# A gated attention unit and a state-space stage, four batches in a hardware loop against four batches unrolled and interleaved

## The chip, the core and the metric

The kernel runs on one core of one Trainium2 chip. Its time is the device time of one execution in microseconds (us). The core has five engines with instruction streams of their own, which meet only at semaphores: TensorE (PE) multiplies matrices into PSUM, VectorE (DVE) and ScalarE (ACT) work element by element, GpSimd (POOL) does some element work too, and SyncE (SP) issues transfers. PE loads weights in a side stream (PEld).

## The reference, cut to what matters

The program chains six blocks on a residual tensor of 4 batches x 1024 tokens x 128 channels. The change touches the third and the fifth. Both normalise twice, and the result of the first normalisation is added to the residual.

```python
x = attention(x); x = x + moe(norm(x))            # blocks 1 and 2, not touched
# block 3, gated unit, per batch b
n = norm(x[b]); x2 = norm(n)                      # the block's own layernorm is the second
u, v, base = split(silu(x2 @ uv_w.T + uv_b))      # 256, 256 and 128 channels
q, k = rope(base * gamma + beta)                  # two affine copies, rotated
kern = relu(q @ k.T / sqrt(128) + toeplitz(w)) ** 2      # 1024 x 1024
x[b] = x[b] + n + (u * (kern @ v)) @ o_w.T + o_b
x = x + moe(norm(x))                              # block 4, not touched
# block 5, state space, per batch b, 16 states
n = norm(x[b]); x2 = norm(n)
xs, z = split(x2 @ W_in.T)                        # 256 channels each
u = silu(causal_conv(xs, 4 taps))
dt, B, C = split(u @ W_xproj.T)                   # 16 + 16 + 16
delta = softplus(dt @ W_dt.T + b_dt)
h[s, t] = exp(delta[t] * A[s]) * h[s, t-1] + delta[t] * B[s, t] * u[t]   # per state s
y = sum_s C[s] * h[s] + D * u
x[b] = x[b] + n + (y * silu(z)) @ W_out.T
# block 6: gated feed-forward, attention, gated feed-forward, not touched
```

## The kernel before

Channels of a block lie on the 128 partitions while it is computed (256 channels are two tiles, c = 0 and 1); the 1024 tokens of a batch run along the free axis, in two halves of 512 (g), since a PSUM bank holds 512 numbers. All eight PSUM banks are one tile `ps`. Most matmuls are float32 and are recorded as two passes of the array, so `x8` in a row of PE is four matmuls.

**Order.** Nothing is scheduled by a planner. Each block has one function per engine, the instructions stand in the order in which the function writes them, and each engine waits on named semaphores (`sm[...]`). Both blocks run in a hardware loop over the four batches (`Fori`, lines 2131 to 2260 build it per engine). At the end of a turn each engine reports to `batch_done`, SP waits for all of them, clears every semaphore of the stage and lets them go on (`finish`, `clear`). So nothing of batch b+1 starts before batch b is wholly done.

**Gated unit** (`pe_gau` L808, `act_gau` L857, `dve_gau` L880, `pool_gau` L931). DVE normalises twice (`dve_layernorm` L82: statistics L79, variance L91, a root on POOL L100, the subtraction and scaling L94), then adds to X (L885, L886). PE transposes eight token tiles (L107), ACT copies them out (L114), PE projects base (L814), gate u (L818), the rotated base (L823) and value v (L827). ACT applies silu (L861, L865) and the two affine copies (L869, L873); DVE adds the bias of v (L889), ACT takes its silu (L877), DVE rotates q and k (L893 to L897). Then come 16 steps u, two for each block j of 128 keys: PE scores (L838), DVE adds the Toeplitz bias (L903) and squares the positive part (L906), and PE multiplies by v (L844), one j behind the scores. At the end DVE gates (L912), PE projects out (L852) and DVE adds to X tile by tile (L921).

**State space** (`pe_mamba` L1267, `act_mamba` L1345, `dve_mamba` L1385, `pool_mamba` L1453). It has the same two normalisations and L1390 for the addition to X, the projections (PE L1274), copies (ACT L1349, L1352), the convolution (DVE L1394, L1398), silu (ACT L1355), low-rank dt and B, C in two matmul groups (PE L1280, L1285), copies of them (ACT L1357, L1359), a split of B and C into three bf16 parts (DVE L1403 to L1407), D*u (DVE L1410), delta (PE L1292, ACT L1362 to L1367, DVE L1415 to L1420). Then 16 states. In each, DVE multiplies by B for c = 0 (`drive`, L1426), POOL for c = 1 (L1465), ACT makes the decays (L1379), DVE scans (L1433, twice) and multiplies by C (L1438, twice), and PE spreads B and C (L1314, L1326) and sums y in PSUM (L1308, `add_y`). `drive` of state n+1 stands right behind the products of state n. POOL's product for a state waits for the scans of the state before and for the sum that frees its buffer. At the end: gate (L1448), output projection (L1340), addition (L921).

## Time and profile before

| | us |
|---|---|
| median of 3 runs (3761.12 to 3766.71) | 3764.24 |
| the profiled execution: its time | 3772.41 |
| the profiled execution: its span | 3769.2 |
| PE busy | 2795.5 (74%) |
| DVE busy | 2229.2 (59%) |
| ACT busy | 1601.7 (42%) |
| POOL busy | 707.9 (19%) |

The blocks follow one another, so the busy shares are averages over stages with different limits. The gated unit lies from 1594 to 1948 us of the span, the state-space stage from 2225 to 3043 us. Together they are 1172 us. A time that an engine sits idle in them counts only where nothing else on the path is running.

### The profile page before, as it was taken

The numbers are of one execution on the slowest core, as the hardware profiler recorded it, in microseconds if no ns is written. First come the engines' busy times: TensorE is split into PE (matmuls) and PEld (weight loads), VectorE is DVE, ScalarE is ACT, GpSimd is POOL, SyncE is SP. The second block draws the span as 40 slices with busy tenths as digits, with TensorE's granted clock in tenths as the row PEclk, the third lists the DMA queues.
The fourth block names the chain that finished last, engine by engine and source line by source line (L and its number), as shares of the span: only waits on it lengthen the run. The fifth ranks groups of instructions, "written<-read, shape, count | busy, mean of one in ns | idle before, by whom it ended". The sixth has DMA issues, their size and how long they took to land.

```text
span 3769.2 us, 55186 instructions
## 1 busy us (share of the span) xinstructions
PE 2795.5 (74%) x18720; PEld 1601.4 (42%) x18720; DVE 2229.2 (59%) x4893; ACT 1601.7 (42%) x2886; POOL 707.9 (19%) x926
## 2 busy tenths in 40 slices
PE   2998899899899926367762636666665688888888
PEld 1666566566566626333332622222222253233225
DVE  2564555455456431355553238889796988777754
ACT  1665566476466502111100314242433333666672
POOL 2000000000000064300016332212121221222221
PEclk9999999999999958688875867778777798999998
DMA  5000000000000011100001210000000034011000
GB/s 157 1 0 2 1 0 1 2 1 0 2 1 0 12 39 52 39 0 0 0 4 39 60 28 0 0 0 0 0 0 0 0 116 157 2 47 47 2 2 23
DMA packets 65897, 78.75 MB, mean 21 GB/s; under 512 B 9005, under 2 KB 41948, under 8 KB 65712
## 3 DMA queue, kind: packets, MB, share of 16 engines
q1 hardware_dynamic: 56816, 60.10, 4.9%
q0 software_dynamic: 8896, 16.29, 1.6%
q8 instruction: 102, 1.67, 0.2%
q14 instruction: 83, 0.68, 0.1%
HBM read 43.58 MB, written 35.52 MB: 21 GB/s over the span
## 4 chain that ended last, share of the span: by engine, by line
PE 28%; DVE 15%; issue 13%; POOL 4%; another core or an unknown queue 3%; ACT 2%; DVEq 0%; DMA 0%; POOLq 0%; SPq 0%; ACTq 0%
DVE Wqkv L1737 4%; PE ps L1613 3%; PE ps L844 3%; PE ps L971 2%; PE ps L590 2%; PE ps L838 2%; PE ps L579 2%; DVE arena L1433 2%; PE ps L1585 1%; DVE arena L1438 1%; POOL arena L1465 1%; PE ps L1574 1%; PE ps L980 1%; POOL slots_in L749 1%
## 5 line engine op out<-in xcount | busy, mean ns | idle before, releaser
L431 DVE CUSTOM_DVE_ANT_0 arena<-ps,causal 128x512 f32<-128x512 f32 (+3 forms) x512 | 282.7, 589 | 345.3 <-PE ps L247 343.8
L355 ACT ACTIVATE arena<-ps 128x512 f32<-128x512 f32 (+1 forms) x640 | 337.8, 548 | 321.7 <-PE ps L260 318.9
L368 ACT ACTIVATE arena<-arena 128x640 f32<-128x640 f32 (+7 forms) x512 | 393.8, 770 | 36.7 <-DVE arena L431 32.7
L1737 DVE TENSOR_REDUCE Wqkv<-ps 128x2 f32<-128x1024 f32 (+3 forms) x384 | 353.3, 953 | 87.1 <-PE ps L1578 81.7
L260 PE MATMUL ps<-ident,arena 128*128 128x128 f32 x2304 | 359.5, 283 | 46.1 <-ACT arena L368 44.6
L1693 ACT ACTIVATE arena<-ps 128x1024 f32<-128x1024 f32 (+3 forms) x384 | 302.3, 809 | 163.0 <-PE ps L1585 159.3
L281 PE MATMUL ps<-arena,rope 128*64 128x128 f32 x4608 | 350.5, 282 | 0.0
L1433 DVE TENSOR_TENSOR_SCAN arena<-arena 128x1024 f32<-128x1024 f32 x128 | 318.9, 2532 | 9.2 <-ACT arena L1379 4.7
L260 PEld LDWEIGHTS ps<-ident,arena 128*128 128x128 f32 x2304 | 249.0, 141 | 177.0 <-issue 144.2
L1308 PE MATMUL ps<-arena,ident 128*128 128x512 f32 x512 | 281.7, 702 | 0.0
L281 PEld LDWEIGHTS ps<-arena,rope 128*64 128x64 f32 x4608 | 242.3, 136 | 74.8 <-issue 64.1
L1465 POOL TENSOR_TENSOR arena<-arena 128x1024 f32<-128x1024 f32 x64 | 150.6, 2353 | 553.4 <-PE ps L1308 218.7
L508 POOL COPY arena<-arena 128x512 f32<-128x512 f32 x64 | 39.5, 616 | 1055.0 <-DVE arena L455 1055.0
L247 PE MATMUL ps<-arena 64*128 64x512 bf16 (+3 forms) x2304 | 233.5, 327 | 5.1 <-ACT rope L347 5.1
L1375 ACT ACTIVATE arena<-ps 128x1024 f32<-128x1024 f32 x64 | 65.5, 1023 | 318.3 <-PE ps L1314 318.3
L1314 PE MATMUL ps<-arena,select 96*128 96x512 bf16 x128 | 51.9, 497 | 182.3 <-DVE arena L1426 182.3
L1308 PEld LDWEIGHTS ps<-arena,ident 128*128 128x128 f32 x512 | 120.7, 236 | 142.6 <-issue 132.7
L1613 PE MATMUL ps<-arena,W 128*32 128x512 f32 (+3 forms) x1536 | 164.5, 500 | 7.2 <-POOL arena L1764 3.6
L763 POOL DMA_INDIRECT arena<-slots_out,arena x128 | 128.2, 1002 | 197.0 <-DMA slots_out<-arena 88.2
L714 DVE TENSOR_SCALAR arena<-ps,b1T 128x160 f32<-128x160 f32 x128 | 42.6, 379 | 203.6 <-remote 112.4
L1585 PE MATMUL ps<-arena 64*128 64x512 bf16 (+3 forms) x768 | 124.8, 334 | 46.4 <-DVE Wqkv L1737 39.5
L100 POOL TENSOR_TENSOR rstd<-var_eps,minus_half 128x8 f32<-128x8 f32 x28 | 46.2, 1650 | 554.4 <-DVE var_eps L91 440.1
(259 smaller groups left out, 4824.0 us busy)
## 6 DMA issues: line engine op xcount, KB each, us to landing
arena<-q_dram SPq DMA_DIRECT2D x4, 2048.0 KB, 8.8
arena<-k_dram SPq DMA_DIRECT2D x4, 2048.0 KB, 14.1
q_dram<-arena SPq DMA_DIRECT2D x24, 256.0 KB, 3.7
k_dram<-arena SPq DMA_DIRECT2D x24, 256.0 KB, 3.8
arena<-slots_in SPq DMA_DIRECT2D x8, 640.0 KB, 4.5
slots_out<-arena SPq DMA_DIRECT2D x8, 640.0 KB, 3.9
slots_in<-arena POOLq DMA_DIRECT2D x4, 640.0 KB, 7.9
W<-in_m_W_dram SPq DMA_DIRECT2D x1, 2048.0 KB, 9.9
```

What stands on the lines that cost most here:

```text
L247: mm = nc.tensor.matmul(k.ps[:, banks[h], 0:w], q, kk, start=part == 0, stop=part == 2)
L260: mm = nc.tensor.transpose(k.ps[:, 4 + m % 2, (b - b0) * P:(b - b0 + 1) * P], k.prob[:, n % 2, h, j * P:(j + 1) * P], k.ident[:])
L281: mm = nc.tensor.matmul(k.ps[64 * h:64 * h + 64, 6 + n // 4, (n % 4) * P:(n % 4 + 1) * P], k.v_tok[:, parity, j, 64 * h:64 * h + 64], k.pr ...
L355: nc.scalar.activation(k.probT[:, n % 2, b0 * P:(b0 + nb) * P], k.ps[:, 4 + m % 2, 0:nb * P], ACT.Copy)\
L368: nc.scalar.activation(k.prob[:, i % 2, h, 0:w], k.prob[:, i % 2, h, 0:w], ACT.Exp, bias=k.neg_max[:, i % 2, h:h + 1], scale=-1.0, accum_o ...
L431: ins = nc.vector.tensor_tensor_reduce(k.prob[:, i % 2, h, 512 * g:512 * g + w], k.ps[:, banks[h], 0:w], k.causal[:, first:first + w], 1.0 ...
L1308: mm = nc.tensor.matmul(k.ps[:, 4 + 2 * c + g, :], k.ident[:], k.h[:, 2 * m + c, g * 512:(g + 1) * 512], start=False, stop=last)
L1433: nc.vector.tensor_tensor_scan(h, k.da[:, 2 * m + c, :], h, 0.0, ALU.mult, ALU.add).then_inc(sm["scan"], 1)
L1465: nc.gpsimd.tensor_tensor(k.h[:, 2 * m + 1, :], k.du[:, 1, :], k.b_row[:, m, :], ALU.mult).then_inc(sm["dbx1"], 1)
L1613: mm = nc.tensor.matmul(k.ps[32 * r:32 * r + 32, 6, 512 - w:512], k.v_aug[b % 2][:, j, 4 * Q + r, :], k.expT[:, (2 * s + a) % 4, h, 0:w], ...
L1693: nc.scalar.activation(k.expT[:, n % 4, :, 0:w], k.ps[:, 2 * (m % 3):2 * (m % 3) + 2, 0:w], ACT.Exp, scale=-1.0)\
L1737: nc.vector.tensor_reduce(k.least[:, g, a, i % 4, c, :], k.ps[:, 2 * (m % 3):2 * (m % 3) + 2, 0:search_width(i, c)], AX_X, ALU.min)\
```

## The change

The hardware loops over batches of the two blocks are gone. Each engine's function now contains all four batches in one straight stream, semaphore counts go on over batches, and there is one `finish` per block. Within that stream:

- The two normalisations of batch b+1 are cut into 16 pieces (`dve_norm_piece`; pieces 3 and 9 are empty, and 14, 15 and, in the state-space stage, 13 hold nothing). Piece n stands behind step n of batch b on DVE. POOL's two roots stand behind states 3 and 9.
- PE transposes and projects batch b+1 around its last sums of batch b; ACT and DVE follow with its copies, rotation or convolution. The output projection of batch b now stands behind projections of b+1.
- Results are added to X in two operations of 512 columns instead of eight of 128, and the output projection waits for all four gated pieces at once.
- State space: dt, B and C come from one group of matmuls (112 rows of weights); D*u moves from DVE to ACT; softplus's logarithm, the addition and the product are done per half. `h`, `conv`, `ud`, `xs` and `XN2s` lie in the space of weights that are no longer needed, and z is double buffered.

Main parts of the diff:

```diff
+def dve_norm_piece(nc, k, dve, ch, sm, b, piece, out):
+    if piece in (0, 1, 6, 7):
+        for t in range(4 * (piece % 2), 4 * (piece % 2) + 4):
+            last = nc.vector.bn_stats(k.bn6[:, t, :], (k.X_all[:, 8 * b + t, :] if piece < 2 else k.XN[:, t, :]))
+        ch.link(last)
+    elif piece in (2, 8):
+        for t in range(8):
+            last = nc.vector.bn_aggr(k.mv[:, t, :], k.bn6[:, t, :])
+        ch.link(last)
+        nc.vector.tensor_scalar(k.var_eps[:], k.mv[:, :, 1], EPS, None, ALU.add).then_inc(sm[("var1", "var2")[piece // 8]], 1)
+    elif piece in (4, 5, 10, 11):
+        dve.wait_ge(sm[("rstd1", "rstd2")[piece // 10]], b + 1)
...
+    elif piece == 12:
+        X = k.X_all[:, 8 * b:8 * b + 8, :]
+        ch.link(nc.vector.tensor_tensor(X, X, k.XN[:], ALU.add))
...
 def pe_gau(nc, k, pe, sm):
...
+    for b in range(k.B):
+        for j in range(8):
+            scores(b, j)
+            if j >= 1:
+                mix(b, j - 1)
+        if b + 1 < k.B:
+            pe.wait_ge(sm["biased"], 16 * b + 14)
+            pe_tokens(nc, k, pe, sm, b + 1, k.XN2)
+        mix(b, 7)
+        if b + 1 < k.B:
+            base(b + 1)
+            gate(b + 1)
+            rotated(b + 1)
+        results(b)
+        if b + 1 < k.B:
+            value(b + 1)
...
 def dve_gau(nc, k, dve, ch, sm):
...
+    def prepare(b):
+        for c in range(2):
+            dve.wait_ge(sm["affine"], 4 * b + c + 1)
+            ch.mark(nc.vector.tensor_tensor(k.gaff[:, c, :], k.gaff[:, c, :], k.cos[:], ALU.mult))
+        for c, dst in enumerate((k.gq, k.gk)):
+            dve.wait_ge(sm["affine"], 4 * b + 3 + c)
+            ch.link(nc.vector.tensor_tensor(k.gaff[:, 2 + c, :], k.gaff[:, 2 + c, :], k.sin[:], ALU.mult))
+            nc.vector.tensor_tensor(dst[:], k.gaff[:, c, :], k.gaff[:, 2 + c, :], ALU.add).then_inc(sm["qk"], 1)
+        if b >= 1:
+            add_results(b - 1)
+        dve.wait_ge(sm["v_ps"], b + 1)
...
             nc.vector.scalar_tensor_tensor(k.kern[:, j, g * 512:(g + 1) * 512], tmp, 0.0, tmp, ALU.max, ALU.mult)\
                 .then_inc(sm["kern"], 1)
-        dve.wait_ge(sm["kern"], u + 1)
+            if b + 1 < k.B:
+                norm_piece(b + 1, u)
...
 def pe_mamba(nc, k, pe, sm):
...
+        if b + 1 < k.B:
+            pe.wait_ge(sm["dbx0"], 16 * b + 16)
+            pe.wait_ge(sm["b"], 16 * b + 16)
+            pe_tokens(nc, k, pe, sm, b + 1, k.XN2s)
+            project(b + 1, 0)
+        add_y(b, NSTATE - 1)
+        if b + 1 < k.B:
+            project(b + 1, 1)
+            project(b + 1, 2)
+            project(b + 1, 3)
+        results(b)
...
 def dve_mamba(nc, k, dve, ch, sm):
...
+    for b in range(k.B):
+        split_bc(b)
+        step_size(b)
+        drive(b, 0)
+        for n in range(NSTATE):
+            step(b, n)
+            if n + 1 < NSTATE:
+                drive(b, n + 1)
+            if b + 1 < k.B:
+                dve_norm_piece(nc, k, dve, ch, sm, b + 1, n, k.XN2s)
+        if b + 1 < k.B:
+            convolve(b + 1, 0)
+        gate(b)
+        if b + 1 < k.B:
+            convolve(b + 1, 1)
+        add_results(b)
...
 def pool_mamba(nc, k, pool, sm):
...
+            if n in (3, 9) and b + 1 < k.B:
+                pool_norm_root(nc, k, pool, sm, b + 1, n // 9)
...
-            with pe.Fori(5, 5 + B) as b:
-                use_batch(k, b - 5)
-                pe_gau(nc, k, pe, k.G)
-                finish(b)
+            pe_gau(nc, k, pe, k.G)
+            finish(5)
```

The end of a batch on PE in the gated unit, before: the last scores and products, the output projection, and the end of the loop's body, whose next turn begins with L107.

```order
L838 MATMUL ps<-arena 128x512 x2
L844 MATMUL ps<-arena 128x512 x8
L852 MATMUL ps<-owT,arena 128x128 x16
L2154 REGISTER_ALU
L2164 REGISTER_ALU
L2164 COMPARE_AND_BRANCH
```

And of the change, where L903 are scores, L912 products with v, L850 the next batch's transposes, L869, L877, L884 and L890 its base, gate, rotated base and value, and L922 the output projection:

```order
L903 MATMUL ps<-arena 128x512 x2
L912 MATMUL ps<-arena 128x512 x4
L850 MATMUL ps<-ident,arena 128x128 x8
L912 MATMUL ps<-arena 128x512 x4
L869 MATMUL ps<-XNT,uvT 128x512 x2
L877 MATMUL ps<-XNT,uvT 128x512 x4
L884 MATMUL ps<-arena,rotate 128x512 x2
L922 MATMUL ps<-owT,arena 128x128 x16
L890 MATMUL ps<-uvT,XNT 128x256 x8
L903 MATMUL ps<-arena 128x512 x4
```

The transposes went ahead of the last four products, three projections ahead of the output projection, and the value projection behind it.

Two states on DVE in the state-space stage, before (a scan is named by its operands here, L1433; L1438 are the products with C, L1426 is `drive`):

```order
L1433 SCALAR_TENSOR_TENSOR arena<-arena 128x1024
L1438 TENSOR_TENSOR arena<-arena,ps 128x1024 x2
L1423 REGISTER_ALU
L1425 ISA
L1426 TENSOR_TENSOR arena<-arena,ps 128x1024
L1430 REGISTER_ALU
L1433 SCALAR_TENSOR_TENSOR arena<-arena 128x1024
```

And of the change, states 1 and 2 of a batch (L1585 scans, L1590 products, L1576 `drive`):

```order
L1585 SCALAR_TENSOR_TENSOR W<-arena,W 128x1024 x2
L1590 TENSOR_TENSOR W<-W,ps 128x1024 x2
L1576 TENSOR_TENSOR W<-arena,ps 128x1024
L816 BN_STATS bn<-X 128x6 x4
L1585 SCALAR_TENSOR_TENSOR W<-arena,W 128x1024 x2
L1590 TENSOR_TENSOR W<-W,ps 128x1024 x2
L1576 TENSOR_TENSOR W<-arena,ps 128x1024
L820 BN_AGGR mv<-bn 128x2 x8
L822 TENSOR_SCALAR var_eps<-mv 128x8
L1585 SCALAR_TENSOR_TENSOR W<-arena,W 128x1024 x2
```

A piece of the next batch's normalisation now stands between `drive` and the next scans.

From the last state of one batch to the first of the next on DVE, of the change (before, L1448 and L921 closed the batch and everything else of these rows stood behind the barrier):

```order
L1590 TENSOR_TENSOR W<-W,ps 128x1024 x2
L1526 TENSOR_SCALAR W<-Wqkv,conv_w 128x1024
L1530 SCALAR_TENSOR_TENSOR W<-Wqkv,conv_w,W 128x1024 x3
L1537 TENSOR_TENSOR W<-ps,arena 128x512 x4
L1526 TENSOR_SCALAR W<-Wqkv,conv_w 128x1024
L1530 SCALAR_TENSOR_TENSOR W<-Wqkv,conv_w,W 128x1024 x3
L1544 TENSOR_TENSOR X<-X,ps 128x512 x2
L1549 TENSOR_TENSOR arena<-ps,arena 32x1024 x2
```

The next batch's convolution (L1526, L1530) now lies on either side of this batch's gate (L1537), ahead of its addition to X (L1544).

## Rows read from the trace of the kernel before

**Rows 1.** Busy time in four stretches: length, PE, PEld, DVE, ACT, POOL; PE clock.
```profile
1675.00:1763.46 88.46, 63.72 (x168) 31.37 (x168) 47.68 (x106) 13.82 (x12) 3.27 (x2) 0.85 0.00 0
1725.00:1764.00 39.00, 38.46 (x90) 16.72 (x88) 19.54 (x29) 0.00 (x0) 0.00 (x0) 1.00 0.00 0
2286.23:2419.88 133.65, 86.98 (x183) 34.37 (x182) 132.50 (x79) 47.35 (x46) 35.33 (x16) 0.79 0.00 0
2419.88:2490.95 71.07, 41.31 (x100) 16.87 (x99) 38.91 (x83) 23.07 (x21) 5.67 (x4) 0.73 0.00 0
```
**Rows 2.** Timeline of DVE, gated unit, second batch: start, busy, [idle before <-releaser].
```profile
1682.70 1.64 DVE L79 BATCH_NORM_STATS2 bn<-X 128x6 f32 x8 [1.00 <-SPq L2058]
...
1686.97 2.14 DVE L94 TENSOR_SCALAR XN<-X,mv,rstd 128x128 f32 x8 [1.75 <-POOL rstd L100]
...
1695.47 1.23 DVE L885 TENSOR_TENSOR X<-X,XN 128x1024 f32 x1
...
1709.67 2.48 DVE L889 TENSOR_TENSOR arena<-ps,uvb_row 128x512 f32<-128x512 f32 x4 [11.71 <-PE ps L827]
...
1716.72 2.36 DVE L897 TENSOR_TENSOR arena<-arena 128x1024 f32<-128x1024 f32 x2
```
**Rows 3.** Timeline of PE, gated unit, second batch.
```profile
1693.83 2.27 PE L107 MATMUL ps<-ident,arena 128*128 128x128 f32 x8 [12.46 <-DVE arena L94]
1696.96 3.78 PE L814 MATMUL ps<-XNT,uvT 128*128 128x512 f32 x4 [0.87 <-ACT XNT L114]
...
1719.14 6.56 PE L838 MATMUL ps<-arena 128*128 128x512 f32 x8 [9.59 <-DVE arena L897]
...
1756.43 7.03 PE L844 MATMUL ps<-arena 128*128 128x512 f32 x16
...
1766.40 3.44 PE L852 MATMUL ps<-owT,arena 128*128 128x128 f32 x24 [0.33 <-DVE X L921]
```
**Rows 4.** Timeline of ACT, gated unit, second batch.
```profile
1700.79 1.11 ACT L861 ACTIVATE arena<-ps,uvb 128x1024 f32<-128x1024 f32 x1 [2.57 <-PE ps L814]
...
1705.43 2.36 ACT L869 ACTIVATE arena<-arena,g_cols 128x1024 f32<-128x1024 f32 x2
...
1712.19 1.91 ACT L877 ACTIVATE arena<-arena 128x2048 f32<-128x2048 f32 x1 [2.20 <-DVE arena L889]
```
**Rows 5.** Timeline of DVE, a step of the first batch.
```profile
1641.63 0.69 DVE L903 SCALAR_TENSOR_TENSOR arena<-ps,toeplitz 128x512 f32<-128x512 f32 x1 [2.28 <-PE ps L838]
```
**Rows 6.** Timeline of DVE, state space, end of batch one to scans of batch two.
```profile
2417.55 2.33 DVE L1438 TENSOR_TENSOR arena<-arena,ps 128x1024 f32<-128x1024 f32 x2
...
2449.41 0.81 DVE L1394 TENSOR_SCALAR arena<-arena,conv_w 128x1024 f32<-128x1024 f32 x1 [5.25 <-ACT arena L1349]
2450.26 3.93 DVE L1398 SCALAR_TENSOR_TENSOR arena<-arena,conv_w 128x1024 f32<-128x1024 f32 x3
...
2471.09 2.47 DVE L1403 TENSOR_TENSOR arena<-ps,arena 32x1024 f32<-32x1024 f32 x2 [12.21 <-ACT arena L1359]
...
2490.95 4.47 DVE L1433 TENSOR_TENSOR_SCAN arena<-arena 128x1024 f32<-128x1024 f32 x2 [1.17 <-ACT arena L1379]
```
**Rows 7.** Timeline of DVE and POOL, two states of the first batch.
```profile
2395.99 4.47 DVE L1433 TENSOR_TENSOR_SCAN arena<-arena 128x1024 f32<-128x1024 f32 x2
...
2403.00 2.35 POOL L1465 TENSOR_TENSOR arena<-arena 128x1024 f32<-128x1024 f32 x1 [7.97 <-PE ps L1308]
...
2403.94 5.74 DVE L1433 TENSOR_TENSOR_SCAN arena<-arena 128x1024 f32<-128x1024 f32 x2
```
**Rows 8.** Timeline of PE, the sums of one such state, and the low-rank matmuls.
```profile
2404.77 3.60 PE L1308 MATMUL ps<-arena,ident 128*128 128x512 f32 x8
...
2460.02 6.37 PE L1280 MATMUL ps<-arena,WxT 128*16 128x512 f32 x8 [6.43 <-ACT arena L1355]
```
**Rows 9.** Timeline of ACT, a table load and the exponential of softplus.
```profile
2475.83 1.28 ACT L1365 ACT_TABLE_LOAD   x1
2477.13 1.91 ACT L1365 ACTIVATE arena<-arena 128x2048 f32<-128x2048 f32 x1
```

734 lines of the change are left out of this document (390 added, 344 removed).

## The prediction, made before the changed kernel was timed

> **What bounds the kernel now.** I read the profile by stages first, because the page's shares mix blocks with different limits. Busy time by stretch [rows 1] shows one period of the gated unit, from the end of one batch's products with v to the next: 88.46 us, of which PE is busy 63.7 and DVE 47.7. Inside its 16 steps PE is busy 38.5 of 39 us at a granted clock of 1.00. So the steps are bound by PE, and the rest of the period is a chain through all engines. The state-space stage is the opposite: in its 16 states DVE is busy 132.5 of 133.65 us, and between the last products of one batch and the first scan of the next lie 71.07 us with DVE busy only 38.9. Then I read the timelines of these gaps to see which wait ends last.
>
> Gated unit [rows 2, 3]: DVE normalises from 1682.7 to 1697.9, PE sits 12.46 us until the first normalised tile, DVE then sits 11.71 us for the value matmuls, and PE 9.59 us for the rotated q and k. State space [rows 6]: DVE waits 5.25 us for the projections and 12.21 us for the low-rank ones. Those are the waits that the change can take away.
>
> **Gated unit, one transition.** Unit costs. PE at full clock takes 7.03 us for 16 passes of 512 columns [rows 3], near 0.43 each: base 1.7, gate 3.4, rotation 1.7, value 3.4 (eight 256-column matmuls, taken as the same number of columns), scores of one j 1.7, its products 3.4. Transposes 2.3, output projection 3.44 for 24 of 32 passes, so 4.6 [rows 3]. ACT takes 1.1 per 1024 columns and 1.9 for v [rows 4]. DVE takes 2.48 for four 512-column pieces, 1.2 per 1024-column product [rows 2], and 1.45 per step, two operations of 0.69 and the gap between them [rows 5].
>
> Let K be the end of a batch's products. The transposes and their copies lie ahead of K, behind products of 3.4. Then PE: base until K+1.7; the gate needs three of four gated pieces, K+1.9 to 5.3; rotation 7.0; output projection 11.6; value 15.1. ACT: base 2.9, two affine copies 5.3, u 7.5, the rotated copies 8.6 and 9.7. DVE: gated 2.5, cosine products 6.5, the sine products and additions end at 13.4, additions to X 14.8, bias of v 17.5; ACT's silu of v ends at 19.5. PE meanwhile does the scores of j = 0 and 1 until 18.5, so it idles about 1 us for v. I add 1 us for the second key half, whose step on DVE waits behind the bias of v and a piece. From there PE needs 3.4 for the first products and 5.15 for each j; the eight products, the seven scores still between them and the transposes end at K+59.6.
>
> Do the pieces delay it? DVE's pieces here are the 15.25 us between 1682.7 and 1697.95, less two root waits of 1.75 [rows 2], about 12 us, at most 2.5 per j beside 2.9 of steps. Only one j reaches 5.4 against PE's 5.15, and DVE has lead by then (it idles 2.28 in each j now [rows 5]). Cost nothing; if that cover is gone, up to 12 us per batch. The roots fall in a step's shadow. The period falls from 88.5 to 59.6: 28.9 x 3 = 87. In the first batch q and k are prepared ahead of v's bias: about 7 less of PE's 9.6 idle. The output projection at the very end no longer streams with the gate: 1 more. **Gated unit: -93.**
>
> **State space, one transition.** E is the end of the last products, 2419.88; the next scan is at E+71.1 [rows 6]. After: PE does tokens and the first projection ahead of the last sum, done at about E+2.4; ACT's copy E+3.5; convolution of c = 0 takes 0.81 and 3.93 [rows 6], 8.2; gate 2.5, 10.7; convolution of c = 1, 15.4; silu 16.5. PE: last sum 5.9, three projections 11.1, output projection 15.7, low rank 19.1 (one group of 3.4 where there were two). ACT: D*u is done by 18.7, dt copy 20.1. PE: delta 21.9 and 23.6. ACT: absolute values 24.7, a table load and the exponential of 1.28 and 1.91 [rows 9], 28.0, another load and the first logarithm, 30.4. DVE: addition and product for both halves, four of 1.2, 35.3; `drive` 36.6. POOL's product started at 35.4 and takes 2.35; it holds the scan as described next, until 37.7. Gain 71.1 - 37.7 = 33.4. The split of B and C, the other long DVE item (it begins near 21.1), ends before the logarithm does.
>
> **State space, the 16 states.** DVE is the limit, so pieces are not free. A state without a disturbance is 7.95 us from scan to scan (2395.99 to 2403.94 [rows 7]). Every second one is longer: its two scans take 5.74 instead of 4.47, while POOL's product, started at 2403.00 after 7.97 us of waiting for PE's sum, still runs until 2405.35, 1.4 us into them [rows 7]. PE is late there because it ran part of that sum at the lower clock: the mean over the states is 0.79 [rows 1], the undisturbed sum takes 3.60 [rows 8]. From first scan to last product 15 x 7.95 + 6.8 = 126 would remain of 133.65; 7.6 are this contention. A piece of 0.8 to 1.2 between `drive` and the scan moves the scan behind POOL's product: two neighbouring pieces add over 1.4 in most states. So the pieces add their work, some 11 us (the gated unit's 12 without L886), and take back about 5.6 of the 7.6 (what is left sits at the empty pieces and the last states). The two roots on POOL, 1.6 each (DVE waits 1.75 for one now [rows 2]), may collide with scans: between 0 and 3.3, I take 1.6 since either may start first; two scaling pieces may meet POOL's product, 0.9. Sum: 126 + 11 + 2 + 1.6 + 0.9 = 141.5, that is 7.9 more. Net per transition 33.4 - 7.9 = 25.5, three of them 76.5; the last batch has no pieces.
>
> The Trainium skill ("SBUF — State Buffer", Who interferes with whom) says that a DVE instruction with two SBUF inputs, or one in a 2-port mode, and a GpSimd instruction that reads SBUF exclude each other for the whole instruction, whoever starts first. The lengthening of 1.27 for 1.41 us of overlap agrees. By that rule a root that starts first holds the scan for all its 1.6 us, against this change: both would always cost, 3.3 a batch, 5 us more in all than my sum.
>
> First batch: from its silu the same chain as above, 60.6 us from start to scan now; the merged low-rank matmuls (6.37 for the first group at the lower clock [rows 8]) and the halves of softplus save about 8.5. The end loses 1.3 like the gated unit. **State space: 76.5 + 8.5 - 1.3, so -83.7.** Everything else (blocks 1, 2, 4 and 6) is as before; the barriers' 1 us each are inside the periods.
>
> **Sum.** 93 + 83.7 = 176.7. The profiled execution, 3772.4 with 3.2 us around its span, would be 3596; it is 8.2 above the median, so the median goes from 3764.2 to **3588**.
>
> **Rivals.** (a) The scans stay held. If every state of the three batches loses 1.27, not only a few, each has 20.3 instead of 2: 3 x 18.3 = 55, so 3643. For it: PE idles longer per state with pieces in it, and its clock was already low in every second state. Against: the pieces shift the scans. 12%. (b) The lower clock in the transitions: 17 us of matmuls per gated transition and 8.5 on the path in state space, doubled, 3 x 25.5 = 77: 3665. For: the matmuls behind idle times of 9 to 12 us are slow now (6.56 for eight passes [rows 3]). Against: idle times before them shrink to 1 or 2 us. 6%. (c) DVE becomes the gated unit's bound and each piece is exposed, 12 x 3 = 36: 3624. 5%. (d) It doesn't overlap as it says: only normalisations, transposes and the barrier leave the path (1681.7 to 1697.0, 15.3 us in either stage [rows 2, 3]), since the next projections wait for this batch's banks. Then each gated transition gains 13.6 less and each of state space 18.1 less: 3 x 31.7 = 95, 3683. 4%. (e) Slower: PE, busy without a pause, is granted only the lower of its two levels, 1.2 GHz, through the gated unit. Its matmuls per batch (41.2 of steps, 17.1 of the rest, 58 us) double: four times 58 = 232 against the gain of 177, 3820. It decides from 76% of that work at the lower level. Against: 1.00 over 39 us of unbroken work [rows 1]. 3%.
>
> **How the numbers follow.** My forecast, 68% (2% are left for what I don't see): its own bounds are -6 for a gated period with no idle at all, -14 if nothing collides in the states, and +19 if the collisions stay as they are (5.6 x 3, with the second root), +15 for hops and leads I took as free: 3568 to 3622. The range takes in (c) and most of (a), to hold 8 in 10: 3566 to 3643. Under 0.2% (7.5 us) a measurement can hardly tell from no change. Faster: all but (e) and a little unknown, 0.95; same 0.01; slower 0.04.
>
> **What would show it.** Gated unit: period near 60, PE idle before the first products 1 to 2 us, clock near 1.00 throughout. State space: first scan 36 to 39 us behind the last product; scans of 4.5 per pair in most states with pieces; a period near 179 against 204.7. The forecast is wrong if DVE idles beyond 2 us for PE in the gated steps, if pairs of scans of 5.7 stay in every second state, or if another chain than silu, low rank and softplus ends last between batches.

## The result and the profile after

The changed kernel took **3555.4 us** (median of 4 runs, 3552.0 to 3556.6) against 3764.1 of the kernel before in the same session: 0.9444 of it, 95% interval 0.9428 to 0.9461. The forecast was 3588 with a range from 3566 to 3643. The direction and the mechanism were right; the gain is 209 us where 177 were forecast, and the time lies 11 us below the range. The same program, timed again in a later session, took 3563.2 (`after_again` below), 3 us below the range.

The profiled execution took 3556.6 (span 3554.6). PE, DVE, ACT and POOL busy, against 2795.5, 2229.2, 1601.7 and 707.9 before:

```profile
PE 2724.2 (77%) x18688; PEld 1583.0 (45%) x18688; DVE 2196.1 (62%) x4845; ACT 1599.9 (45%) x2891; POOL 717.9 (20%) x923
```

The number of matmul passes is nearly the same (18720 before), and PE is busy 71 us less. TensorE's granted clock has two levels in these traces, 1.00 (2.4 GHz) and 0.50 (1.2 GHz). Eight passes of 512 columns take 3.60 us at the full level and about 7.2 at the lower one (the row of after_again at the end of this text); a time between the two means that the level changed on the way, and a granted clock between the two is a mean over a stretch. Less of PE's work ran at the lower level after the change, and most waits went. Busy time by stretch, the answer to [rows 1] (length, PE, PEld, DVE, ACT, POOL, clock): a period of the gated unit, the states of the second batch, its transition to the third (last product to first scan), and the states of the last batch, which hold no pieces:

```profile
1666.84:1724.90 58.06, 56.51 (x170) 28.56 (x169) 45.78 (x100) 11.14 (x10) 3.27 (x2) 1.00 0.00 0
2342.57:2479.85 137.28, 86.69 (x196) 35.52 (x197) 136.56 (x130) 48.30 (x48) 43.64 (x18) 0.85 0.00 0
2479.85:2513.29 33.44, 26.42 (x78) 12.01 (x78) 26.27 (x27) 24.16 (x22) 1.10 (x1) 0.85 0.00 0
2683.98:2819.58 135.60, 88.01 (x185) 35.12 (x186) 134.05 (x79) 46.44 (x45) 36.55 (x16) 0.79 0.00 0
```

The gated unit is now bound by PE, 56.5 of 58.06 us. The transition fell from 71.07 to 33.44. The states rose by 3.6 only, though 11 pieces went into them; and the last batch, without pieces, is hardly shorter.

Where the 214.6 us between the two profiled spans are, from the boundaries of the stages on DVE:

| stretch | before | after | gain | forecast |
|---|---|---|---|---|
| up to the gated unit (block 2 is 281.5 / 277.8 of it) | 1594.9 | 1591.1 | 3.9 | 0 |
| gated unit | 353.3 | 256.7 | 96.6 | 93 |
| block 4 | 277.5 | 273.4 | 4.1 | 0 |
| state space | 818.5 | 710.1 | 108.4 | 83.7 |
| the rest | 725.0 | 723.3 | 1.7 | 0 |

PE in the second transition of the gated unit, the answer to [rows 3] (L850 transposes, L912 products with v, L869, L877, L884 and L890 base, gate, rotation and value, L922 output projection):

```profile
1720.43 1.04 PE L850 MATMUL ps<-ident,arena 128*128 128x128 f32 x8
1721.30 3.60 PE L912 MATMUL ps<-arena 128*128 128x512 f32 x8
...
1726.88 3.70 PE L877 MATMUL ps<-XNT,uvT 128*128 128x512 f32 x8 [0.26 <-DVE arena L1021]
...
1732.13 3.73 PE L922 MATMUL ps<-owT,arena 128*128 128x128 f32 x32
...
1744.05 1.13 PE L912 MATMUL ps<-arena 128*128 128x512 f32 x2 [1.29 <-ACT arena L970]
```

The waits of 12.46 and 9.59 us in [rows 3] are now one of 1.29. The eight transposes take 1.04 where 2.27 stood.

The transition from the second to the third batch of state space, E = 2479.85, all engines (L1526 and L1530 convolution, L1537 gate, L1374 low rank, L1490 copy of dt, L1386 delta, L1563 the first addition of softplus, L1585 scans):

```profile
2479.43 1.02 ACT L1479 ACTIVATE Wqkv<-ps 128x1024 f32<-128x1024 f32 x1 [2.07 <-PE ps L1366]
2480.49 0.81 DVE L1526 TENSOR_SCALAR W<-Wqkv,conv_w 128x1024 f32<-128x1024 f32 x1 [0.64 <-ACT Wqkv L1479]
...
2485.18 2.48 DVE L1537 TENSOR_TENSOR W<-ps,arena 128x512 f32<-128x512 f32 x4
...
2493.49 1.97 PE L1374 MATMUL ps<-arena,WxT 128*112 128x512 f32 x4 [0.16 <-ACT arena L1485]
2495.53 1.02 ACT L1490 ACTIVATE arena<-ps 16x1024 f32<-16x1024 f32 x1
2496.60 3.80 PE L1386 MATMUL ps<-arena,WdtT 16*128 16x512 f32 x8 [1.15 <-ACT arena L1490]
...
2507.17 1.23 DVE L1563 TENSOR_TENSOR arena<-arena 128x1024 f32<-128x1024 f32 x1 [1.89 <-ACT arena L1500]
...
2513.29 3.40 DVE L1585 TENSOR_TENSOR_SCAN W<-arena,W 128x1024 f32<-128x1024 f32 x1
```

E is again the end of the last product. DVE waits 0.64 us for the projection where it waited 5.25 [rows 6]. The chain through silu, low rank and softplus ends last, as forecast, but it starts at E+0.6, not E+3.5.

DVE, POOL and PE in the states, the answer to [rows 7, 8]: first a state with a piece, then the fourth state, whose scans have a root on POOL beside them, then a held pair of scans in the last batch (L816 a piece, L842 a root, L1632 POOL's product, L1405 the sum):

```profile
2351.44 0.86 DVE L816 BATCH_NORM_STATS2 bn<-X 128x6 f32<-128x128 f32 x4
2352.33 4.47 DVE L1585 TENSOR_TENSOR_SCAN W<-arena,W 128x1024 f32<-128x1024 f32 x2
...
2369.52 4.47 DVE L1585 TENSOR_TENSOR_SCAN W<-arena,W 128x1024 f32<-128x1024 f32 x2
...
2369.69 3.55 POOL L842 TENSOR_TENSOR rstd<-var_eps,minus_half 128x8 f32<-128x8 f32 x1 [1.72 <-DVE var_eps L822]
...
2694.67 5.28 PE L1405 MATMUL ps<-W,ident 128*128 128x512 f32 x8
...
2700.12 2.36 POOL L1632 TENSOR_TENSOR W<-arena 128x1024 f32<-128x1024 f32 x1 [8.08 <-PE ps L1405]
...
2700.98 5.83 DVE L1585 TENSOR_TENSOR_SCAN W<-arena,W 128x1024 f32<-128x1024 f32 x2
```

With a piece the scans start behind POOL's product and take 4.47. Without pieces the old pattern is back. The root did not hold a scan: it began 0.17 us behind the first of the two and took 3.55 us itself, where one without a scan beside it takes 1.64.

### The profile page after: what moved, and what is told of

It reads as the page before. It is cut to its first block, busy times and chain, and to the rows that moved or that the text cites. A ratio compares the mean times of both kernels' runs of the same rounds, so it can differ in the third digit from the quotient of the medians.

```text
span 3554.6 us, 53842 instructions
## 1 busy us (share of the span) xinstructions
PE 2724.2 (77%) x18688; PEld 1583.0 (45%) x18688; DVE 2196.1 (62%) x4845; ACT 1599.9 (45%) x2891; POOL 717.9 (20%) x923
## 4 chain that ended last, share of the span: by engine, by line
PE 25%; DVE 17%; issue 13%; another core or an unknown queue 3%; ACT 3%; POOL 2%; DMA 0%; DVEq 0%; POOLq 0%; SPq 0%; ACTq 0%
DVE Wqkv L1902 4%; PE ps L1778 3%; PE ps L912 3%; PE ps L1070 2%; DVE W L1590 2%; PE ps L590 2%; DVE W L1576 2%; PE ps L579 2%; PE ps L1750 2%; PE ps L903 1%; PE ps L1739 1%; DVE W L1585 1%; POOL slots_in L749 1%; PE ps L1079 1%
## 5 line engine op out<-in xcount | busy, mean ns | idle before, releaser
L368 ACT ACTIVATE arena<-arena 128x640 f32<-128x640 f32 (+7 forms) x512 | 393.9, 770 | 36.8 <-DVE arena L431 33.3
L1585 DVE TENSOR_TENSOR_SCAN W<-arena,W 128x1024 f32<-128x1024 f32 x128 | 303.0, 2408 | 3.9
L1405 PE MATMUL ps<-W,ident 128*128 128x512 f32 x512 | 276.9, 692 | 0.0
L1632 POOL TENSOR_TENSOR W<-arena 128x1024 f32<-128x1024 f32 x64 | 150.6, 2353 | 497.4 <-PE ps L1405 203.6
L1405 PEld LDWEIGHTS ps<-W,ident 128*128 128x128 f32 x512 | 118.9, 232 | 137.9 <-issue 129.0
L1590 DVE TENSOR_TENSOR W<-W,ps 128x1024 f32<-128x1024 f32 x128 | 148.7, 1203 | 0.0
```

The lines of the kernel that those rows point to most:

```text
L368: nc.scalar.activation(k.prob[:, i % 2, h, 0:w], k.prob[:, i % 2, h, 0:w], ACT.Exp, bias=k.neg_max[:, i % 2, h:h + 1], scale=-1.0, accum_o ...
L1405: mm = nc.tensor.matmul(k.ps[:, 4 + 2 * c + g, :], k.ident[:], half(k.h[:, 2 * (n % 2) + c, :], g), start=False, stop=n == NSTATE - 1)
L1585: nc.vector.tensor_tensor_scan(h, k.da[:, 2 * (n % 2) + c, :], h, 0.0, ALU.mult, ALU.add).then_inc(sm["scan"], 1)
L1590: nc.vector.tensor_tensor(h, h, both(k.ps[:, 2:4, :]), ALU.mult).then_inc(sm["prod"], 1)
```

## Experiments

The runs fell on three chips. On two of them (13 and 14) blocks 2 and 4 take 206.0 to 208.9 us each in every kernel, on chip 9 273.4 to 281.5, and the kernel before takes 3624 and 3764. The other stages differ less (the gated unit of the change is 255.2 to 256.7, the part behind state space 723.2 to 725.1), so small effects are read from the length of a stage. The change itself was not run on 13 or 14. "The change" without a session means the 710.1 us of state space above, and "states" and "transition" are the two parts of a batch there: first scan to last product, and last product to the next batch's first scan.

### The two stages apart

`g_only` is the kernel before with the new functions of the gated unit and one `finish`; `s_only` is the changed kernel with the old ones and their loop.

> The gated unit of the change in the kernel before, state space as before. Theory (the two stages are independent, and the gated unit gave what the two traces show, 353.3 us before against 256.6 after): 3764 - 97 = 3667 us, and the second mixture-of-experts block behind it stays at 277.5 us. By the prediction's own term (93) it would be 3671. Rival: the 4.1 us by which that block was shorter in the changed kernel (273.4) belong to the unrolled gated unit in front of it; then 3663 and the block near 273.4.

> The state-space stage of the change with the gated unit as before. Theory: the stage takes 710 us instead of 818.5, so 3764 - 108 = 3656. By the prediction's own term (83.7) it would be 3680. Rival: what was gained beyond the forecast comes from one kernel's luck in alignment between stages, or from outside the stage; then between 3660 and 3680.

Measured in one session (before 3762.6): g_only 3670.9, ratio 0.9753 (0.9737 to 0.9769); s_only 3655.8, 0.9715 (0.9699 to 0.9731). The gains are 91.7 and 106.9, together 198.6. That is 10 us short of the 208.7 of the change, but it lies outside the two stages: these are 256.7 and 710.2 us long, as in the change. So they are independent, and most of the missed gain is inside state space. Block 4 is 276.1 with the new gated unit and 275.0 with the old one; in six later runs of kernels with the new one on this chip it is 273.5 to 276.5, and the change's own is 273.4 in its first session and 276.4 in after_again. So its 4.1 us, and block 2's 3.7, do not belong to the change: they vary from run to run.

### The cover taken away

```diff
# s_tokens_late                                  # state space, PE
-            pe_tokens(nc, k, pe, sm, b + 1, k.XN2s)
-            project(b + 1, 0)
         add_y(b, NSTATE - 1)
+            pe_tokens(nc, k, pe, sm, b + 1, k.XN2s)
+            project(b + 1, 0)
# g_pieces_late                                  # gated unit, DVE, behind the loop over u
-            if b + 1 < k.B:
-                norm_piece(b + 1, u)
+        if b + 1 < k.B:
+            for piece in range(14):
+                norm_piece(b + 1, piece)
```

> The changed kernel, but the next batch's transposes and first projection stand behind the last sum of the states instead of ahead of it. Theory: convolution begins 0.6 us after the last product now because tokens, copy and projection lie in the last state's shadow. Behind the sum they come one after another (sum until 3.0 us after the last product, transposes and first copy 2.1, projection 2.0, copy 1.1), convolution begins at 8.2, and nothing else covers it: 7.6 x 3 = 23 slower than 3555, 3578; with PE at its lower level there up to 3584. Rival: another chain (the gate, the output projection, the low-rank matmuls) ends late anyway and hides most of it; then under 10 slower, 3565 or less.

> The changed kernel, but in the gated unit the next batch's normalisation stands in one piece behind step 16 instead of one piece behind each step. Theory (the pieces cost nothing among the steps, because DVE idles there for PE): 13.5 us of pieces and two waits of 1.75 for a root are laid bare, less 3.6 that the products before the last cover, 13 us per batch, 39 in all: 3594, up to 3603 if PE falls to its lower level behind them. Rival: DVE was the bound in the steps with pieces, which cost about as much there as at the end; then within 12 of 3555.

s_tokens_late: 3588.7, 0.9536 (0.952 to 0.9552). The transition is 43.3 instead of 33.4, with E = 2491.20:

```profile
2495.42 1.04 PE L850 MATMUL ps<-ident,Wo 128*128 128x128 f32 x8
...
2500.64 0.81 DVE L1526 TENSOR_SCALAR W<-Wqkv,conv_w 128x1024 f32<-128x1024 f32 x1 [9.44 <-ACT Wqkv L1479]
```

Convolution starts at E+9.4, 8.8 us later than in the change, and the next scan comes 9.9 later: nothing hides the delay. The sum in front took 5.37 us for its eight passes, part of them at the lower level, which is the step from the expected 7.6 to 8.8. The last 1.1 are not in the start of the convolution: the output projection took 5.44 where the change has 3.80, and the low-rank matmuls stood behind it. The whole run is 33 us slower than the change, more than the expected 23 to 29. Of the 33.8 in state space 29.7 are the transitions and 3.6 the states, which are up to 2.4 us longer per batch; why was not followed up.

g_pieces_late: 3602.6, 0.9569 (0.9553 to 0.9585). The gated unit is 293.6 against 256.7, 12.3 per batch, as the forecast had it ("up to 12"), and DVE waits 1.75 for each root again, with PE idle. The whole run is 47 us above the change; besides these 37 us, 4.5 are a longer state-space stage (714.6, as in after_again, see "Not settled") and the rest lies in the untouched blocks. The transposes behind the idle time:

```profile
1743.72 2.05 PE L850 MATMUL ps<-ident,arena 128*128 128x128 f32 x8 [10.79 <-DVE arena L829]
```

So in the gated unit pieces are free among the steps. The transposes took 2.05 behind that idle time, 1.04 in the change.

### What holds the scans

```diff
# sum_split                                      # PE, in each state n
     for n in range(NSTATE):
+        if n >= 1: add_y(b, n - 1, (1,))        # c = 1 first
         if n + 1 < NSTATE: spread_b(b, n + 1)
         spread_c(b, n)
-        if n >= 1: add_y(b, n - 1)
+        if n >= 1: add_y(b, n - 1, (0,))
# drive waits for y_acc 2N - 2, POOL's product for 2N - 3
```

So POOL's product for c = 1 needs only the first half of PE's sum.

`before_sum_split` is the same edit in the kernel before.

> The changed kernel, but in each state PE sums the products of c = 1 first, then spreads B and C, then sums c = 0; POOL's product waits for the first half of the sum only. Theory (a scan is held because POOL's product starts late, and it starts late because PE, at 1.2 GHz after an idle time, ends the sum of eight passes behind the scans): every product of POOL now starts with the end of the scans and is over before the next ones. The last batch, which has no pieces, loses 8 holds of 1.2 (135.6 us from its first scan to its last product become 126 to 127.2), the three others 2.3 each: 15 to 16 us less than 3555, 3540. Rival 1: the lateness has another cause (the copy of B, the scans themselves): no change, 3555. Rival 2: spreading C later makes the products with C wait: slower, up to 3565.

> The kernel before with the same new order of PE's sums in the states (loops, barriers, everything else as before). Theory: 133.65 us of states become 126 to 127, four times 6.6 to 7.6: 3764 - 28 = 3736. If pieces were what really freed the scans in the change, and PE's order has no part in it, then no change: 3764. It also says what the pieces cost in truth: with the holds gone in both kernels they should cost their own 9 to 10 us per batch.

before_sum_split: 3594.2, 0.9915 (0.9899 to 0.9932) of 3623.9, 29.6 less. Its states of the second batch, and below them those of sum_split (last batch, second batch):

```profile
2336.94:2462.51 125.57, 86.45 (x183) 33.26 (x182) 124.43 (x79) 47.34 (x46) 35.44 (x16) 0.83 0.00 0
```

```profile
2552.51:2679.60 127.09, 81.13 (x185) 31.47 (x186) 125.54 (x79) 46.43 (x45) 36.63 (x16) 0.89 0.00 0
2209.28:2344.99 135.71, 84.80 (x191) 33.04 (x191) 134.99 (x130) 47.88 (x47) 43.69 (x18) 0.86 0.00 0
```

133.7 became 125.6 without any piece, and the last batch of the change 135.6 became 127.1. Each pair of scans takes 4.47 us now, but for the first of each batch in sum_split (5.57): the scans were held because POOL's product waited for PE's sum. With the holds gone the pieces show their real price, 135.71 - 127.09 = 8.6 us per batch. In the change they cost 1.7 beside the last batch (137.28 against 135.60), since they take the holds back.

But sum_split is only 3415.4, 0.9422 (0.9407 to 0.9438), and its stage 706.6: 3.5 us less where 15 to 16 were expected. The states gave back 13.2; the transitions took 7.9 (36.4, 37.8 and 34.0 instead of 33.4) and the end 1.8. Of the 7.9, about 2 only follow from where E lies: the last scans are no longer held (4.47 instead of 5.04), E comes 0.6 earlier, and PE's part does not, so convolution starts at E+1.3. The other 6 are PE's clock: in the second transition the half sums ahead of the transposes took 2.77 and 2.42 us instead of 1.98 and 1.88 (convolution at E+3.0), and delta took 6.12 and 5.86 us in the first two transitions where the change has 3.80:

```profile
2364.08 5.86 PE L1386 MATMUL ps<-arena,WdtT 16*128 16x512 f32 x8 [1.15 <-ACT arena L1492]
```

So part of the gain in the states was lost again to a lower clock of PE on the path. Whether it can be held up, the next runs ask.

### The order of the gate and a table load

```diff
# gate_last                                      # DVE
             convolve(b + 1, 0)
-        gate(b)
-        if b + 1 < k.B:
             convolve(b + 1, 1)
-        add_results(b)
+        gate(b)
# PE: results(b) and DVE: add_results(b) behind the next batch's delta
# exp_early                                      # ACT, behind the copy of B and C
+        nc.scalar.activation(k.warm[:], k.minus_half[:, 0:1], ACT.Exp)
```

> The changed kernel, but in the state-space stage this batch's gate (2.5 us of DVE) stands behind both halves of the next batch's convolution, and its output projection and addition to X behind delta. Theory: convolution, silu, low rank, delta and softplus are the chain that ends last between batches, and the gate lies on it with its whole 2.5 us: 3 x 2.5 = 7.4 less, 3548. Rival 1: another chain (sum, gate, output projection, addition to X) ends as late: no change, or slower by up to 3 x 3 = 9, since the output projection now stands ahead of the first B of the batch: 3555 to 3564.

> The changed kernel with one more ACT instruction per batch: an exponential of one column behind the copy of B and C, so that the table load of 1.28 us falls in ACT's idle 1.0 us before delta instead of between the absolute values and the exponential. Its result is not used. Theory: the chain through softplus is the last one; 1.28 is taken off it and the idle time before delta covers all of it but 0 to 0.5: 4 x 0.8 to 1.28 = 3.2 to 5.1 less, 3550 to 3552. Rival: the absolute value brings back another table, so the load returns where it was: no change or 5 slower, 3555 to 3560.

gate_last: 3419.6, 0.9433 (0.9418 to 0.9449); stage 710.2, transitions 33.4: no change. Its low-rank matmuls and the copy of dt were earlier, with 2.15 us of idle time of PE before the one and 1.11 behind them; delta started at E+15.0 instead of E+16.8, and then took 5.46:

```profile
2359.83 5.46 PE L1386 MATMUL ps<-arena,WdtT 16*128 16x512 f32 x8 [1.11 <-ACT arena L1493]
```

exp_early: 3417.3, 0.943 (0.9415 to 0.9446); stage 706.8. ACT's load lies under PE's delta, and the exponential of 1.91 follows the absolute value directly:

```profile
2189.31 1.28 ACT L1492 ACT_TABLE_LOAD   x1
2190.60 0.20 ACT L1492 ACTIVATE arena<-minus_half 128x1 f32<-128x1 f32 x1
...
2193.18 1.91 ACT L1498 ACTIVATE arena<-arena 128x2048 f32<-128x2048 f32 x1
```

The way to the first scan of the stage is 1.3 shorter, as expected, and the transitions are 32.6, 31.3 and 33.5. But delta took 5.14 in the third, and the states of the first three batches are 2.2 us longer in all (137.8, 138.9 and 137.4): from first scan to first scan the batches are 170.5, 170.2 and 170.9 long, where the change has 170.8, 170.7 and 170.7. So what the transitions gained was given back in the states; the 3.3 us of the stage are the 1.3 up to the first scan, 0.6 in these three batches and 1.4 in the states of the last one.

### PE's clock

Six kernels, counting the combinations, fill PE's idle time with matmuls whose result is zero or unused.

```diff
# warm: 32 rows, bf16, 8 passes behind each sum  # warm_rows: 128 rows, float32, 4 passes
+  nc.tensor.matmul(k.ps[:, 4 + i % 4, :], zeros32, zeros32, start=False, stop=False)
+  nc.tensor.matmul(k.ps[:, 4 + i % 4, :], k.ident[:], k.nil[:], start=False, stop=False)
# gate_last_warm: zeros of 32 rows               # gate_last_full: data, 128 rows
#   ahead of low_rank (8 or 4 passes) and ahead of delta (4 or 2)
# zeros32 stands for slices of rows 96 to 127 of `select`, which hold zeros
+  nc.tensor.matmul(k.ps[:, bank, :], zeros32, zeros32, start=True, stop=True)
+  nc.tensor.matmul(k.ps[:, bank, :], k.WinT[:, 0:P], half(k.XNT, 0), start=True, stop=True)
```

`all3` is warm, gate_last_warm and exp_early; `after_again` is the changed kernel beside them.

> The changed kernel itself, once more, on the same chip as the three runs beside it, so that differences of a few microseconds can be read directly. On the first chip it was 0.9444 of the kernel before. The other chip runs the two mixture-of-experts blocks 140 us faster for every kernel; if this is that chip, 3623.9 - 208 = 3416 and 0.943 to 0.944, with 710 us for the state-space stage.

> The changed kernel with matmuls of zeros in PE's idle time within the states: behind each state's sum 8 passes of 512 columns of zeros are added to the sums (20 in the first state). They change nothing in the result and add 1.7 us of work per state. Theory (every second sum runs at 1.2 GHz because PE idled 4 to 5 us before it, so POOL's product is late, and it holds the scan): with the idle time filled the clock stays at 2.4 GHz, the granted clock of the states rises from 0.85 and 0.79 to above 0.95, all sums take 3.6, the last batch's states fall from 135.6 to 127, the other three from 137.3 to 135.7, and the transitions stay at 33.4, since the last sums are at full clock anyway: 13 us less than the changed kernel beside it. Rival: the clock alternates whatever PE does, or zeros don't count as work: the passes then lengthen the slow states, 0 to 20 us more.

> gate_last (the gate behind both convolutions, the output projection behind delta) with matmuls of zeros into a free PSUM bank while PE waits for silu (8 passes) and for the copy of dt (4 passes). gate_last alone brought nothing: its second silu ended 1.9 us earlier behind the last product, but delta took 5.46 instead of 3.80 us at the lower clock. Theory (that clock swallowed the gain): delta is back at 3.8, transitions fall from 33.4 to about 31.5, three times 1.9, and the first batch, which has such a wait too, by up to 1: 5 to 7 us less than the changed kernel beside it. Rival: the output projection ahead of the first B of the batch, or the softplus chain of ACT, ends last now: within 2 of the changed kernel.

> The zeros in the states, gate_last_warm and exp_early together. If the three act on different terms (holds of scans 13, order of the gate 6, one table load 1.2 x 4 = 4.8) they add up: 24 us less than the changed kernel beside it. If the gate's order and the table load share one chain whose end is then DVE's split of B and C (it ended 1.2 us ahead of the logarithm in exp_early), 3 to 4 of it are lost: 20 less.

Measured on chip 9 (before 3764.4): after_again 3563.2, 0.9464 (0.9448 to 0.948); warm 3558.6, 0.9452 (0.9436 to 0.9468); gate_last_warm 3556.2, 0.9446 (0.943 to 0.9461); all3 3558.5, 0.9455 (0.944 to 0.9471). The three are 4.6, 7.1 and 4.7 us below after_again, but about 4 of that is chance: after_again's state space is 714.6 us long, 3.6 of it a slower way to the first scan, and the stages of the three are 710.7, 710.4 and 711.7, like the 710.1 of the change's first session. So the expected gains (13, 5 to 7 and 20 to 24) did not come. The zeros of 32 rows are in the trace as busy time, yet sums of 5.4 go on among sums of 3.6 (the last batch's states fell to 132.5 at a granted clock of 0.88, not to 127), and in gate_last_warm delta behind such a filler, with 0.14 us of idle time before it, still took 5.39:

```profile
2718.89 5.40 PE L1405 MATMUL ps<-W,ident 128*128 128x512 f32 x8
2724.22 1.90 PE L1411 MATMUL ps<-select 32*128 32x512 bf16 x8
```

```profile
2495.37 1.03 PE L1371 MATMUL ps<-select 32*128 32x512 bf16 x4
2495.47 1.02 ACT L1499 ACTIVATE arena<-ps 16x1024 f32<-16x1024 f32 x1 [0.17 <-PE ps L1379]
2496.51 1.02 ACT L1500 ACTIVATE arena<-ps 96x1024 bf16<-96x1024 f32 x1
2496.54 5.39 PE L1392 MATMUL ps<-arena,WdtT 16*128 16x512 f32 x8
```

(The first two rows are of PE in warm, the others of all engines in gate_last_warm.) But in all3 the same delta behind the same filler took 3.69, in all three transitions:

```profile
2492.01 1.03 PE L1371 MATMUL ps<-select 32*128 32x512 bf16 x4
2493.18 3.69 PE L1392 MATMUL ps<-arena,WdtT 16*128 16x512 f32 x8
```

The granted clock says why. In gate_last_warm it fell 1.86 us after delta began, in all3 only when delta was over:

```profile
2496.54:2498.40 1.86, 1.86 (x5) 0.88 (x6) 0.84 (x1) 0.99 (x1) 0.00 (x0) 1.00 0.00 0
2498.40:2501.93 3.53, 3.53 (x6) 0.99 (x4) 3.40 (x5) 1.11 (x1) 0.00 (x0) 0.50 0.00 0
```

(Both rows are of gate_last_warm.) Its transitions are 33.3 and those of all3 32.0, but all3's states with pieces are 138.6 instead of 137.3. So a microsecond in the place of delta decides what it costs, and delta's time alone does not tell what a filler does. Three of the next four runs try filler on all rows; split_exp has none.

> As warm, but the filler behind each sum is two float32 matmuls of a 128-row identity with zeros (4 passes; 10 passes in the first state), where warm had 8 passes of 32 rows. The result is unchanged. Theory A (the clock follows PE's work, and 32 rows of zeros count little): slow sums of 5.2 vanish, the last batch's states fall from 135.6 to 127 to 129, the others from 137.3 to about 136: 10 to 13 us less than after_again (3563 on chip 9, ratio 0.9464), ratio near 0.943. Theory B (zeros never count, whatever the rows): as warm, which was 4 less; sums alternate between 3.6 and 5.2 still. Theory C (the alternation has nothing to do with idle time): the same as B or slower.

> gate_last with real 128-row float32 matmuls (the next batch's first projection again, into a free bank) as filler: 4 passes while PE waits for silu, 2 while it waits for the copy of dt. gate_last and gate_last_warm both had delta at 5.4 instead of 3.8 us and transitions of 33.3 as in the changed kernel. Theory A: with real work on all rows delta is back at 3.8 and the transitions fall to 31.5: 6 us less than the changed kernel, ratio 0.9445 where that is 0.9460. Theory C (delta, of 16 rows, is slow for another reason than what stood before it): delta stays at 5.4, and the transitions at 33.3.

> sum_split and exp_early together. On one chip they were 3415.4 and 3417.3 where the changed kernel should have been 3419 (0.9434); each took 3.5 us off the state-space stage (706.6 and 706.8 against 710.2). If they act on different terms (held scans; one table load per batch) the stage takes 703, 7 us less than the changed kernel; if PE's clock in the transitions, which cost sum_split 8 of its 13, decides both, anything from 698 to 708.

> sum_split, filler of 128-row zeros behind each sum, gate_last_full and exp_early together. If theory A holds in both places: states 127 in the last batch and 135.7 in the others, transitions 33.4 - 1.9 - 1.2 = 30.3, stage about 710 - 13 - 9 - 1 = 687, 23 us less than the changed kernel beside it. If fillers don't hold the clock up (B or C): as split_exp, or slower by what the fillers cost, stage 700 to 712.

Chip 13, before 3624.2: warm_rows 3414.0, 0.942 (0.9404 to 0.9436), stage 703.0; gate_last_full 3414.6, 0.9422 (0.9406 to 0.9438), 703.4; split_exp 3412.1, 0.9422 (0.9406 to 0.9437), 699.7; best 3399.3, 0.9383 (0.9368 to 0.9399), 689.8. Rows of the last batch's states of warm_rows, then one of its sums there with the filler; then delta behind a filler of 128 rows in gate_last_full:

```profile
2546.95:2675.57 128.62, 99.56 (x250) 41.69 (x251) 127.07 (x79) 46.45 (x45) 36.62 (x16) 0.97 0.00 0
```

```profile
2582.23 3.60 PE L1405 MATMUL ps<-W,ident 128*128 128x512 f32 x8
2585.66 1.88 PE L1411 MATMUL ps<-arena,ident 128*128 128x512 f32 x4
```

```profile
2356.68 1.02 PE L1371 MATMUL ps<-XNT,WinT 128*128 128x512 f32 x2
...
2357.94 3.69 PE L1392 MATMUL ps<-arena,WdtT 16*128 16x512 f32 x8 [0.25 <-ACT arena L1499]
```

The same 1.9 us of filler per state, on all rows, keeps the granted clock of the last batch's states at 0.97 where the change has 0.79 and warm 0.88, all its sums but the first take 3.6, and the states fall from 135.6 to 128.6 with PE's order untouched. In the batches with pieces it does less: the second has five more sums of 4.4 to 6.0 (granted clock 0.90 where the change has 0.85), and its states are 136.8 instead of 137.3.

In gate_last_full delta is at 3.7 and the transitions are 31.6: the gain of gate_last was there and the clock had eaten it. The granted clock is 1.00, 0.95 and 1.00 over the three transitions, where gate_last_warm has 0.90: in two of them it did not fall at all. In the states zeros were enough; in the transition only data was tried. Besides the rows, the fillers differ in the type of number (bf16 against float32); which of the two decides was not tried, and in the transitions, after all3, it is not shown that either does.

split_exp took 10.4 off the stage where its parts took 3.5 and 3.3: its states are those of sum_split, its transitions 34.4, 36.6 and 34.9 and its end 10.3, so its last sums and deltas met the clock differently (delta took 3.70, 5.90 and 5.84). Without a filler such small sums could not be forecast here to better than some microseconds.

best holds all of it together (states of the second batch, transition, last batch's states), and DVE in that transition (L1567 the split of B and C, L1603 scans):

```profile
2201.03:2336.75 135.72, 108.53 (x260) 43.94 (x261) 134.99 (x130) 47.89 (x47) 43.72 (x18) 0.94 0.00 0
2336.75:2368.28 31.53, 28.55 (x86) 14.28 (x85) 26.27 (x27) 24.76 (x23) 1.10 (x1) 0.95 0.00 0
2535.53:2662.61 127.08, 100.15 (x251) 41.09 (x252) 125.54 (x79) 46.45 (x45) 36.58 (x16) 0.99 0.00 0
```

```profile
2353.40 2.47 DVE L1567 TENSOR_TENSOR arena<-ps,arena 32x1024 f32<-32x1024 f32 x2 [3.04 <-ACT arena L1508]
...
2368.28 3.40 DVE L1603 TENSOR_TENSOR_SCAN W<-arena,W 128x1024 f32<-128x1024 f32 x1
```

Stage 689.8 against 710.1: 20.3 less, 23 expected. The missing part is the transition, 31.5 instead of 30.3. Half of the 1.2 is again where E lies: the last scans are not held, so convolution starts at E+1.3 instead of E+0.6. The other half is DVE: in gate_last_full it idles 0.59 us between the split and the scan, so no more was left for the table load to save, and in best it has no idle time there. best has the lowest ratio and the shortest stage of all runs.

## Why the prediction was right in kind and short in size

**Gated unit, -93, measured -96.6.** Period 58.06, forecast 59.6. PE waits once, 1.29 us, for the silu of v, as forecast; the pieces are free, and 12.3 when laid bare. Three terms were mis-sized. The transposes take 1.04, not 2.3: that price came from a row behind 12.46 us of idle time [rows 3], at the lower level. The output projection takes 3.73, not 4.6: in its row [rows 3] PE stopped after every eight passes for DVE's addition to X ([0.33 <-DVE X L921]), and these stops were counted as work; the passes themselves take the same 0.11 us in both kernels. And the 1 us for the second key half did not come: the first products start at K+19.2, not K+20.5. The sum was also added up wrongly: from K+20.5 the eight products, the six scores between them (the text says seven) and the transposes end at K+60.5, not K+59.6. The first batch gained 4.3, not 7 (from its first statistics to the end of its products it takes 75.8 instead of 80.1), and the end lost 0.3, not 1. So part of the agreement of 93 with 96.6 is luck: the three periods gained 5.9 more than forecast, the first batch 2.7 less.

**State space, -83.7, measured -108.4.** The period from last product to last product is 170.7, forecast 179.2; the 8.5 us are these terms:

| term, per batch | forecast | measured | from |
|---|---|---|---|
| start of convolution after E | 3.5 | 0.6 | trace of the change |
| the chain from there to the first scan, without the hold | 33.1 | 32.8 | same |
| base of the 16 states | 126 | 126.0 | sum_split's last batch, 127.1 with a hold of 1.1 |
| pieces and the scaling pieces' share | 11.9 | 8.6 | sum_split |
| roots on POOL | 1.6 | 0 | trace: the root waited, the scan did not |
| holds that stay | 2 | 1.6 | 137.3 - 135.7, the change against sum_split |
| first hold by POOL's product | 1.1 | 1.1 | scans of 5.57 |

Two steps failed. In the transition it is "PE does tokens and the first projection ahead of the last sum, done at about E+2.4". In the change they are done at E-0.5: the sum ahead of the transposes took 3.60 us (full level) and the transposes 1.04. The prediction does not show how it came to E+2.4; transposes at its 2.3 and that sum at the 5.1 to 5.3 of the lower level would make up the 2.9. s_tokens_late shows that a later start of convolution arrives whole at the next scan. In the states the failed step is "the pieces add their work, some 11 us", with the roots priced at 1.6 beside it: a piece also fills part of the gap that stands between `drive` and a scan anyway (2394.68 to 2395.99 in the kernel before is 1.31 us for a `drive` of 1.2). In sum_split four statistics recorded as 0.86 lengthen a state by 0.71, and all eleven pieces together cost 8.6. The rest of the stage: the first batch gained 10.0, not 8.5; the last batch's states grew by 1.9, which the forecast had at 0; the end lost 1.8, not 1.3.

**The mechanism of the holds** was read rightly: POOL's product late because of a sum at the lower level, pieces as spacers. The two sum_split runs show that the late product holds the scans, and warm_rows that it is late because of the clock. What the forecast did not see is how regular it is: the last batch shows a hold in every second state for as long as nothing disturbs it.

**The rule of the Trainium skill** ("SBUF — State Buffer", Who interferes with whom) would have made both roots cost 3.3 a batch if they started first. The trace agrees that the later one waits: each of the six roots began 0.17 us behind a scan and took 3.55 us instead of 1.64, and that scan was not lengthened. With an exclusion for the whole instruction it agrees only in part, since the root is recorded 1.5 us into the second scan, which also took its usual 2.27. A root beginning ahead of a scan did not occur, so neither the 3.3 of the rule's other case nor the 1.6 of the sum was paid.

**Rivals.** (a) Scans stay held: not in the batches with pieces, though the last batch kept its holds. (b) The lower clock in the transitions: the other way; the granted clock there rose from 0.73 to 0.85. It is real as a risk: sum_split lost about 6 us to it, and gate_last the 5.4 that gate_last_full then showed. (c) DVE as the gated unit's bound: no, PE is busy 56.5 of 58.06 us. (d) No: projections and convolution of the next batch do overlap, as the rows above show. (e) No: the clock was 1.00 in the gated period.

**The sum.** 3.6 and 24.7 us were short in the two stages. The profiled execution before was 8.2 us above its median, the one after 1.2, and blocks 2 and 4 account for 7.8 of the difference in spans. The last two nearly cancel, so of the 32 us that the forecast was off, 28 lie in the two stages: 9 are the start of convolution (2.9 per transition), 15 the pieces and roots of the states (3.3 and 1.6 per batch), 6 the gated periods, and the small terms left over take about 1 back. The range was too narrow on this side because its lower bound (-6 and -14) let only the waits and the collisions shrink, and held the price of the pieces and the start of convolution fixed.

**Not settled.** The first batch's lead in state space is not fixed: 50.6 us to the first scan in the change, 54.2 in after_again and g_pieces_late, with delta at 3.69 in the first and at 7.19 in after_again (its row below). The change and after_again are the same program; what puts PE on one level or the other there was not found. With 0.8 us in the first batch's states and 3.0 in block 4 it makes most of the 7.8 us between the two sessions.

```profile
2159.52 7.19 PE L1386 MATMUL ps<-arena,WdtT 16*128 16x512 f32 x8 [1.11 <-ACT arena L1490]
```

## What to carry to other kernels

Price a moved matmul at the clock of the place to which it goes, not at that of its row: an overlap that removes PE's idle time also makes the work beside it cheaper, and a rearrangement that opens a wait on PE can lose its whole gain to the clock, or keep it when its work comes to lie a microsecond elsewhere (all3). When an engine is the bound, look at what lengthens its operations (here a GpSimd product that waited for one sum) before counting what is added to it; a reordering of the late engine may be worth more than the spacer that hides it. And read each stage's gain from its own boundaries, since the other stages drift by some microseconds.
